# The last 1x1 convolution of a vision tower written with tokens as rows, with both norms and the gating logits taken from centred weights

## What is computed

```python
# tokenizer: patch embedding and a wavelet branch, gated, then three depthwise + 1x1 pairs
h = relu(dwconv(h, f1_dw, f1_pw, f1_pwb))
h = relu(dwconv(h, f2_dw, f2_pw, f2_pwb))
h = dwconv(loc + h, f3_dw, f3_pw, f3_pwb)          # 3x3 depthwise, then 1x1 with bias
t = transpose(h.reshape(B, D, -1), (0, 2, 1))
t = (t - mean(t)) / sqrt(var(t) + 1e-5) * ln_g + ln_b
h = concatenate([cls, t], axis=1)                  # 37 tokens an image
# the 37 tokens are all queries; there are no keys, so attention adds 0 @ proj_w.T + proj_b
h = layernorm(h + (zeros @ proj_w.T + proj_b))
v = clip(h @ v_w + v_b, -3, 3)                     # feeds a recurrence over the 37 tokens
logits = h @ gate_w + gate_b                       # 8 experts, the best two of each token
# experts: gelu(h @ w1[e] + b1[e]) @ w2[e] + b2[e], weighted; plus bk_scale * spectral part
h = layernorm(h + ffn(h))
```

## Time and profile before

| | |
|---|---|
| device time, median of 3 runs (lowest to highest) | 216.5 us (216.4 to 216.51) |
| the profiled execution: device time / span | 215.94 us / 214.1 us |
| busy: PE, DVE, ACT, POOL | 163.6, 103.6, 48.4, 84.0 us |
| DVE's last depthwise instruction ends | 74.57 us |
| DVE starts the logits (L698) | 93.59 us |
| first product of the experts starts (L998) | 118.29 us |
| granted clock of PE, mean | 0.891 |

### The profile page before, as it was taken

The page is one execution under the profiler, slowest core; times in us unless marked ns, Lnnn a source line. Parts: engine busy times, 40 slices in busy tenths (PEclk is TensorE's granted clock), DMA queues, the critical chain, the costliest instruction groups (busy, mean ns, idle before and its releaser), DMA issues.

```text
span 214.1 us, 2877 instructions
## 1 busy us (share of the span) xinstructions
PE 163.6 (76%) x934; PEld 132.9 (62%) x934; DVE 103.6 (48%) x304; ACT 48.4 (23%) x90; POOL 84.0 (39%) x203
## 2 busy tenths in 40 slices
PE   0999998977998872762207899999999999999100
PEld 0677764444555441562103799999999999999000
DVE  1109897699889949456800042322222223301385
ACT  0453343433311120233000222222221222221000
POOL 1699600000000013101775787878877323322111
PEclk9999999999999996555556999999999999999855
DMA  6992299999991000000222900000012100001412
GB/s 200 334 412 83 59 279 297 297 267 287 282 349 50 0 0 2 0 0 0 100 98 77 312 31 3 0 0 3 2 38 77 55 18 21 18 18 40 148 40 85
DMA packets 13632, 23.47 MB, mean 110 GB/s; under 512 B 1531, under 2 KB 10000, under 8 KB 13490
## 3 DMA queue, kind: packets, MB, share of 16 engines
q1 hardware_dynamic: 10862, 18.74, 28.4%
q0 software_dynamic: 1248, 2.76, 3.8%
q10 hardware_dynamic: 1508, 1.80, 2.6%
HBM read 17.98 MB, written 5.31 MB: 109 GB/s over the span
## 4 chain that ended last, share of the span: by engine, by line
PE 68%; DVE 11%; DMA 7%; POOL 5%; issue 5%; ACT 1%; POOLq 0%; DVEq 0%; ACTq 0%
PE ps L998 20%; PE ps L1008 15%; PE ps L845 8%; PE ps L853 7%; PE ps L854 5%; PE ps L899 5%; POOL slot_rows L405 4%; PE ps L833 3%; DMA w1t_s<-in_w1t 2%; DVE stats L642 2%; DVE conv L596 2%; DMA diag_s<-slot_results 2%; DVE conv L608 1%; POOL rstd L393 1%; DMA slot_rows<-sent,slots 1%
## 5 line engine op out<-in xcount | busy, mean ns | idle before, releaser
L998 PE MATMUL ps<-conv 128*128 128x128 f32 x384 | 45.7, 276 | 1.2 <-ACT conv L526 0.9
L998 PEld LDWEIGHTS ps<-conv 128*128 128x128 f32 x384 | 44.8, 192 | 1.9 <-ACT conv L526 1.4
L596 DVE SCALAR_TENSOR_TENSOR conv<-conv,vecs 128x240 f32<-128x240 f32 (+1 forms) x94 | 35.7, 443 | 7.9 <-ACT conv L463 7.4
L1008 PE MATMUL ps<-w_s,conv 128*128 x192 | 33.7, 326 | 0.0
L393 POOL TENSOR_TENSOR rstd<-var,neghalf 128x2 f32<-128x2 f32 (+1 forms) x6 | 4.9, 813 | 70.6 <-DVE var L648 70.6
L1008 PEld LDWEIGHTS ps<-w_s,conv 128*128 128x128 f32 x192 | 30.9, 190 | 0.0
L791 DVE COPY arena<-ps 128x192 f32<-128x192 f32 x16 | 5.7, 357 | 46.5 <-PE ps L1008 39.3
L413 POOL DMA_INDIRECT slot_results<-arena,home x16 | 17.5, 1091 | 25.5 <-DVE arena L791 23.2
L526 ACT COPY conv<-ps 128x256 f32<-128x256 f32 x16 | 6.0, 372 | 74.9 <-PE ps L989 74.9
L853 PE MATMUL ps<-conv,pw_s 128*128 128x288 f32 (+1 forms) x48 | 17.4, 445 | 5.5 <-DVE conv L608 3.8
L777 DVE COPY conv<-w_s 128x1536 f32 x16 | 15.6, 978 | 6.1 <-issue 6.0
(11 more groups left out here) (158 smaller groups left out, 188.5 us busy)
## 6 DMA issues: line engine op xcount, KB each, us to landing
w_s<-in_w SPq DMA_DIRECT2D x8, 576.0 KB, 14.8
w_s<-in_w SPq DMA_DIRECT2D x8, 384.0 KB
slot_rows<-zero SPq DMA_DIRECT2D x1, 2048.0 KB, 22.7
arena<-in_x SPq DMA_DIRECT2D x4, 432.0 KB, 9.5
w_s<-in_w SPq DMA_DIRECT2D x8, 192.0 KB
pw_s<-in_pw SPq DMA_DIRECT2D x1, 1152.0 KB, 11.4
arena<-slot_rows SPq DMA_DIRECT2D x1, 1024.0 KB, 8.0
w1t_s<-in_w1t ACTq DMA_DIRECT2D x1, 576.0 KB, 4.9
```

Of the source, the lines that this page charges most:

```text
L596: ins = nc.vector.scalar_tensor_tensor(out=o, in0=a, scalar=w, in1=o, op0=ALU.mult, op1=ALU.add)
L998: last = mm(p1_ps[i % 2][:, c * P:(c + 1) * P], w1_cur[:, i % 2, k * F + c * P:k * F + (c + 1) * P], xs[:, i % 2, k * P:(k + 1) * P], star ...
L1008: last = mm(y_ps[i % 2], hT[:, i % 2, k * P:(k + 1) * P], w2_flat[:, bass.ds(expert[i] * (FK * D) + k * D, D)], start=(k == 0), stop=(k == ...
```

## The change

The last 1x1 convolution no longer gives channels as rows that are then turned. The depthwise output `act_b` (tokens as columns) becomes the stationary operand and the weights the moving one, so that tokens come out as rows. Since a layer norm subtracts the mean over channels, the kernel subtracts it from the weights instead (`token_weights` on DVE, seven instructions, run in step (0, 0)). `wt` then holds three parts: the centred weights with a column for the epsilon (`CEN` = 193 columns), the centred weights times the gain, centred again (192), and these times the gate weights (9). The first norm's inverse deviation comes from the sum of squares of the first product (ACT, `Square` with an accumulated sum), and the second's from the sum of squares of `zc` = product times root plus `base` (the shift plus the attention bias, centred). The logits are `raw_ps` (nine more columns of the second product) times the first root, plus `base` times the gate weights (`s2`), times the second root. `bn_stats`, the turns of `act_a` and of `ht`, and the products L947 and L948 are dropped. ACT writes the ten tiles of `sent`. To prepare this PE turns `wt` and `base` with `shared` (the class tokens' row; four turns each) and multiplies them with the gate weights (eight products), between steps of the tokenizer; a row of ones in `act_b`, written by POOL, carries the bias of the convolution. The attention bias takes two products, after `branches`. `xf` has four tiles of columns, `full_tiles` shares the memory of `lgt`, POOL's memsets are five more, and DVE has two for `unit`.

```diff
+CEN, LGT = D + 1, 2 * D + 1
+TW = LGT + E + 1
...
+        tok_rows = [slice(0, min(P, NPX - t * P)) for t in range(NT)]
+        cen_ps = [ps[:, b, o:o + CEN] for b, o in ((0, 0), (0, 256), (2, 0), (3, 0), (4, 0))]
...
+        raw_ps = (psf[:, 512:1024].rearrange("p (t c) -> p t c", t=2)[:, :, D:TW - CEN], ps[:, 5:8, D:TW - CEN])
+        wturn_ps = (ps[:, 2, 0:2 * P], ps[LO, 3, 0:2 * P])
+        bturn_ps = (ps[:, 6, 0:2 * P], ps[LO, 7, 0:2 * P])
+        attn_ps = ps[:, 3, 0:D]
+        wl_ps = ps[:, 0, 0:4 * (E + 1)].rearrange("p (k e) -> p k e", k=4)
...
-            for k, grp in enumerate((0, 0, 1, 1)):
-                inverse_root(k, grp)
+            pool.wait_ge(padded, 11)
+            pool.wait_ge(pw_ev, 12)
+            nc.gpsimd.memset(act_b[DB:DB + 1, 1, :], 1.0).then_inc(ones_row, 1)
+            cr = slice(LAST, LAST + B)
+            pool.wait_ge(d_rows, 16)
+            pool.wait_ge(attn_rdy, 1)
+            pool.wait_ge(d_cls, 16)
+            pool.wait_ge(ones_row, 1)
+            nc.gpsimd.tensor_tensor(base[:], rowb[:, D:2 * D], attn[:], ALU.add).then_inc(base_rdy, 1)
+            pool.wait_ge(base_rdy, 1)
+            nc.gpsimd.tensor_tensor(shared[cr, :], cls_s[cr, :], attn[cr, :], ALU.add).then_inc(base_rdy, 1)
+            pool.wait_ge(bsum_rdy, 2)
+            nc.gpsimd.tensor_scalar(bsum[:], bsum[:], 1.0 / D, None, ALU.mult).then_inc(base_rdy, 1)
+            pool.wait_ge(base_rdy, 3)
+            nc.gpsimd.tensor_scalar(base[:], base[:], bsum[:, 0:1], None, ALU.subtract).then_inc(base_rdy, 1)
+            pool.wait_ge(base_rdy, 4)
+            nc.gpsimd.tensor_scalar(shared[:, :], shared[:, :], bsum[:, 1:2], None, ALU.subtract).then_inc(base_rdy, 1)
+            pool.wait_ge(base_rdy, 5)
+            for k, (c, ts, done) in enumerate(((0, slice(0, 2), 2), (1, slice(0, 2), 4), (0, slice(2, NT), 7),
+                                               (1, slice(2, NT), 10))):
+                if k:
+                    pool.wait_ge(root_rdy, k)
+                pool.wait_ge(sq_rdy, done)
+                nc.gpsimd.tensor_tensor(root[:, c, ts], sq[:, c, ts], neghalf[:, ts], ALU.pow).then_inc(root_rdy, 1)
             pool.wait_ge(d_clear, 16)
-            pool.wait_ge(padded, 6)
-            pool.wait_ge(ht_rdy, NT)
-            pool.wait_ge(copied, 1)
+            pool.wait_ge(padded, 11)
+            pool.wait_ge(copied, 2 * NT)
...
             branches(0)
             branches(1)
-            for f in range(3):
-                for g in range(2):
-                    fusion(f, g)
+            act.wait_ge(attn_mm, 1)
+            nc.scalar.copy(attn[:], attn_ps).then_inc(attn_rdy, 1)
+            fusion(0, 0)
+            act.wait_ge(wturn_mm, 1)
+            nc.scalar.copy(xf[:, 0, 0:2 * P], wturn_ps[0]).then_inc(xf_rdy, 1)
+            nc.scalar.copy(xf[LO, 1, 0:2 * P], wturn_ps[1]).then_inc(xf_rdy, 1)
+            fusion(0, 1)
+            act.wait_ge(bturn_mm, 1)
+            nc.scalar.copy(xf[:, 0, 2 * P:], bturn_ps[0]).then_inc(xf_rdy, 1)
+            nc.scalar.copy(xf[LO, 1, 2 * P:], bturn_ps[1]).then_inc(xf_rdy, 1)
+            fusion(1, 0)
+            fusion(1, 1)
+            act.wait_ge(wl_mm, 1)
+            nc.scalar.copy(wt[:, :, LGT:TW], wl_ps[:, 0:2, :]).then_inc(wl_rdy, 1)
+            nc.scalar.copy(s2[:], wl_ps[:, 2:3, :].to_broadcast([P, NT, E + 1])).then_inc(wl_rdy, 1)
+            act.wait_ge(wl_rdy, 2)
+            nc.scalar.copy(s2[LAST:LAST + B, NT - 1, :], wl_ps[LAST:LAST + B, 3, :]).then_inc(wl_rdy, 1)
...
+            scale = D ** -0.5
+            act.wait_ge(padded, 11)
+            def square(c, t, src, rows_):
+                nc.scalar.activation(sq_out[rows_, c, t, :], src, ACT.Square, scale=scale,
+                                     accum_out=sq[rows_, c, t:t + 1]).then_inc(sq_rdy, 1)
+            for g, tiles in enumerate(groups):
+                for t in tiles:
+                    act.wait_ge(cen_mm, max(t + 1, 2))
+                    square(0, t, cen_ps[t][tok_rows[t]], tok_rows[t])
+                for t in tiles:
+                    act.wait_ge(zc_rdy, t + 1)
+                    square(1, t, zc[:, t, :], A)
+            for c in range(2):
+                for t in range(NT):
+                    act.wait_ge(root_rdy, 2 if t < 2 else 4)
+                    nc.scalar.activation(sent[:, c, t, 0:D], zc[:, t, 0:D], ACT.Copy,
+                                         scale=root[:, 1, t:t + 1]).then_inc(copied, 1)
...
+            def token_weights():
+                last = pw_s[:, 5]
+                gain = rowb[:, 0:D].unsqueeze(1).to_broadcast([P, 2, D])
+                dve.wait_ge(d_pw, 16)
+                dve.wait_ge(d_rows, 16)
+                link(nc.vector.tensor_reduce(wsum[:, 0, :], last, AX.X, ALU.add))
+                link(nc.vector.tensor_scalar(wsum[:, 0, :], wsum[:, 0, :], 1.0 / D, None, ALU.mult))
+                link(nc.vector.tensor_tensor(wt[:, :, 0:D], last, wsum[:, 0, :].unsqueeze(2).to_broadcast([P, 2, D]),
+                                             ALU.subtract))
+                link(nc.vector.tensor_tensor(wt[:, :, CEN:LGT], wt[:, :, 0:D], gain, ALU.mult))
+                link(nc.vector.tensor_reduce(wsum[:, 1, :], wt[:, :, CEN:LGT], AX.X, ALU.add))
+                link(nc.vector.tensor_scalar(wsum[:, 1, :], wsum[:, 1, :], 1.0 / D, None, ALU.mult))
+                nc.vector.tensor_tensor(wt[:, :, CEN:LGT], wt[:, :, CEN:LGT],
+                                        wsum[:, 1, :].unsqueeze(2).to_broadcast([P, 2, D]), ALU.subtract).then_inc(wt_rdy, 1)
...
+                    if (f, g) == (1, 0):
+                        dve.wait_ge(base_rdy, 2)
+                        nc.vector.tensor_reduce(bsum[:, 0:1], base[:], AX.X, ALU.add).then_inc(bsum_rdy, 1)
+                        nc.vector.tensor_reduce(bsum[:, 1:2], shared[:, :], AX.X, ALU.add).then_inc(bsum_rdy, 1)
...
+                        if g == 0:
+                            token_weights()
...
+            dve.wait_ge(base_rdy, 5)
+            for k, tiles in enumerate(groups):
+                dve.wait_ge(root_rdy, 2 * k + 1)
+                for t in tiles:
+                    r = tok_rows[t]
+                    dve.wait_ge(tok_mm, max(t + 1, 2))
+                    nc.vector.scalar_tensor_tensor(out=zc[r, t, 0:D], in0=tok_ps[t][r, 0:D], scalar=root[r, 0, t:t + 1],
+                                                   in1=base[r, :], op0=ALU.mult, op1=ALU.add).then_inc(zc_rdy, 1)
+            def per_token(c):
+                return root[:, c, :].unsqueeze(2).to_broadcast([P, NT, E + 1])
+            dve.wait_ge(wl_rdy, 3)
+            for k, ts in enumerate((slice(0, 2), slice(2, NT))):
+                own(nc.vector.tensor_tensor(lgv[:, ts, :], raw_ps[k], per_token(0)[:, ts, :], ALU.mult))
+            dve.wait_ge(v_done, n)
+            link(nc.vector.tensor_tensor(lgv[:], lgv[:], s2[:], ALU.add))
+            dve.wait_ge(root_rdy, 4)
+            link(nc.vector.tensor_tensor(lgv[:], lgv[:], per_token(1), ALU.mult))
+            own(nc.vector.tensor_tensor(lg[:], lgv[:, :, 0:E],
                                         rowb[:, 2 * D:2 * D + E].unsqueeze(1).to_broadcast([P, NT, E]), ALU.add))
-            nc.vector.tensor_tensor(vt[:], lg_ps[:, :, E:E + 1].to_broadcast([P, NT, P // HB]),
+            dve.wait_ge(d_misc, 16)
...
-                if g == 0:
-                    pe.wait_ge(attn_rdy, 1)
...
-            mm(ps[:, 3, 0:D], zero[:, 0:P], proj_s[:, 0, :], start=True, stop=False)
-            mm(ps[:, 3, 0:D], zero[LO, 0:P], proj_s[LO, 1, :], start=False, stop=False)
-            mm(ps[:, 3, 0:D], ones[:], projb_s[:], start=False, stop=True).then_inc(attn_mm, 1)
             pe.wait_ge(d_pw, 16)
             branches(0)
             branches(1)
-            for f in range(3):
-                for g in range(2):
-                    if (f, g) in PE_HELPS:
-                        taps(f, g)
-                    fusion(f, g)
-            for group, done in (((0, 1), 22), ((2, 3, 4), 24)):
-                pe.wait_ge(pw_ev, done)
-                if group[0] == 0:
-                    pe.wait_ge(d_misc, 16)
-                for t in group:
+            pe.wait_ge(d_proj, 32)
+            pe.wait_ge(zeroed, 1)
+            pe.wait_ge(unit_rdy, 2)
+            mm(attn_ps, zero[:, 0:P], proj_s[:, 0, :], start=True, stop=False)
+            mm(attn_ps, unit[:], proj_s[:, 1, :], start=False, stop=True).then_inc(attn_mm, 1)
+            pe.wait_ge(ones_row, 1)
+            fusion(0, 0)
+            taps(0, 1)
+            pe.wait_ge(attn_rdy, 1)
+            pe.wait_ge(wt_rdy, 1)
+            for k in range(2):
+                nc.tensor.transpose(wturn_ps[0][:, k * P:(k + 1) * P], wt[:, k, CEN:CEN + P], id_s[:])
+                last = nc.tensor.transpose(wturn_ps[1][:, k * P:(k + 1) * P], wt[:, k, CEN + P:LGT], id_s[:])
+            last.then_inc(wturn_mm, 1)
+            fusion(0, 1)
+            pe.wait_ge(xf_rdy, 2)
+            taps(1, 0)
```

(51 more changed lines are left out.)

126 lines of the change are left out of this document (55 added, 71 removed).

## The result

The changed kernel took **209.6 us** in the median of four runs (207.0 to 210.8), beside 216.45 us of the kernel before on the same chip: a ratio of 0.964, 95% interval 0.956 to 0.973. It is faster; 207.6 us was predicted, with a range from 205.4 to 211.3. The runs lie apart: 207.0, 209.6, 209.6 and 210.8. The profiled execution is the one of 210.8 us, so its trace holds losses that a typical run has only in part.

The account below looks back on a forecast made before the run. No engine is full in the 19.02 us relay of latencies from tokenizer to logits; it becomes 7.75: 11.3 gained, 2.4 given back ahead, 8.9 net, 216.5 to 207.6 us, range 205.4 to 211.3.

Parts of the forecast that it names:

- Part 1: Weights prepared on DVE in step (0, 0): seven instructions, 3.25 us against 2.89 idle; +0.1 us into f = 1.
- Part 2: Turns and reductions between tokenizer steps: reductions fit DVE's idle 0.81 us; four turns at 0.23 each make PE 0.45 us late.
- rival (c): PE hides its weight loads, 0.65 us a pair; DVE ends the tokenizer, the turns fit: 205.6 us, chance 0.08.
- Part 3: Eight nine-column products ahead of `fusion(1, 1)`: 1.75 us plus 0.1 wait; that 1x1 starts 1.9 us late, at 65.2.
- Part 4: Token rows of group 0: four pairs at 0.85 us, 3.4 in all; PE ends the tokenizer 2.4 us later.
- Part 5: New relay from tokenizer to logits: squares 0.5 us each, logits at 84.7; stage 7.75 us instead of 19.02.
- a sign of being wrong: Listed in the prediction: it is wrong if the square's accumulated sum on ACT is a second instruction of its own.
- Part 6: Behind the logits: ten copies end near 88.4 us, exponential near 89.9, nothing delays the scatter; warm-up shifts along.
- Rival (e): PE's clock rises later before the experts; missing by 3 us loses 1.5 us: 209.1 us, chance 0.06.
- Rival (g): PE's clock falls to half inside the tokenizer through gaps behind new waits: near 230 us for five half steps, chance 0.04.
- that part moves as a block with whatever releases it: From the first expert product on, PE multiplies back to back, nothing the change touches lies there; that part only shifts.

Follow-up runs that it names:

- again: The changed kernel measured once more with nothing changed: 208.48 us, ratio 0.962; its trace is of the run of 207.19 us.
- 5: Kernel of 4 with POOL's addition for `base` held back until ACT's first copy of step (0, 0): 206.67 us, ratio 0.957.
- 9: Kernel of 4 with turns of `base`/`shared` and four gate products moved later, their additions on DVE in (1, 0), reductions in (1, 1): 204.19 us.
- experiment 7: Changed kernel with the long warm-up of 3, logits made the old way behind the last root, prepared turns and gate products removed: 212.56 us, ratio 0.981.
- 3: Changed kernel with PE's warm-up before the experts of eleven products instead of three, six between the loads of expert numbers: 207.49 us, ratio 0.955.
- 4: Changed kernel with the eleven-product warm-up of 3 and the eight gate products reading 107 columns instead of nine: 206.41 us, ratio 0.955.
- 12: Kernel of 9 plus twelve one-column memsets on POOL that nothing waits for: 205.10 us, ratio 0.946.

## Why the prediction was right, and where it was not

The forecast of faster and the range held, and 207.6 was 2.0 us low. Two errors stand against each other in that. From (0, 0) to the logits the change gained 10.4 us without the dent, for 8.9 forecast: up to the end of the tokenizer it took 29.31 us in "again" (46.06 to 75.37) for 30.28 (46.67 to 76.95), and from there to the logits 7.30 for 7.75. Behind the logits 2.2 to 3.1 us were lost, where the prediction took all as constant, and the dent, where it came, took 1.65. So that the middle of the range came near is in part luck.

- **Part 1.** The seven instructions took 0.55, 0.17, 0.56, 0.56, 0.55, 0.17, 0.56, as estimated; L725 starts at 39.58, 0.41 after L624 in the earlier trace rows (0.35 forecast). POOL's row of ones was ready 0.3 us before (0, 0) needed it. What was missed is beside it: POOL's addition of `base` and its overlap with DVE, 0.6 us (experiments 5 and 9). No term of the sum had it.
- **Part 2.** The four turns stand 0.11 to 0.16 us apart, not 0.23. The clock doesn't explain it: it was full at that row too (1.00 from 77 to 78 us before the change), but there each turn of 128 rows alternates with one of 64, 0.26 and 0.20 apart. What makes the difference is open. The turns fitted into PE's free time, 5.35 us from (0, 1) to (1, 0) for 5.34 before, so the 0.45 was not paid, as rival (c) had it. From (0, 0) to (1, 0) it took 11.65 us, for 11.82 forecast; what was paid there is the overlap of part 1.
- **Part 3.** Eight products in 1.81 us for 1.75 forecast. The 1x1 of (1, 1) started at 65.38 for 65.2, and 6.66 us behind that of (1, 0), for 6.7. The price was right; what it did to the clock was not foreseen.
- **Part 4.** Pairs of token rows start 0.66 to 0.73 apart, not 0.85, close to rival (c)'s 0.65. Four pairs took 2.75 us up to the taps, 0.65 less than forecast, the three of the relay some 0.3 less, at 0.74 to 0.80. DVE had no idle time before its last additions (77.17 above), so DVE ended the tokenizer, and not PE: that too is rival (c), which had 0.08 and a stage shorter by 10.9 us. It was nearer to the stage's 10.4 than the sum's 8.9.
- **Part 5.** The square is 0.33 to 0.36 and its accumulated sum a second instruction of 0.18 to 0.20, which the prediction had named as a sign of being wrong. It cost nothing beyond the 0.5 taken: the second starts before the first ends, so the pair is done after 0.42 to 0.46 us, and the next square starts 0.33 to 0.36 after the one before. Logits at 85.32 in the trace with the dent, 82.67 in that without, for 84.7.
- **Part 6.** The copies ended at 87.88, 3.7 us before the slots; the squares needed no table load, and the one for the exponential began at 87.90. The Trainium skill ("ScalarE: Activation LUTs", section "Table sets: the hidden batching unit") would have asked for one before the squares, as square is not among the functions it names for every set; the trace has none there. The 0.7 us of the slower scatters stood in no term.
- **Rival (e), the clock's later rise,** had 0.06 and came true in both traces of the changed kernel: the first expert group took 5.49 and 4.51 us, 1.6 to 2.6 more than 2.94. It was argued from a single trace, in which the warm-up ended 0.65 us ahead of the rows. The shorter relay by itself moves the warm-up and the rows alike. But counted from the logits the warm-up began at 18.85 us, and at 19.30 before, and the rows came at 24.5 to 24.6, and at 23.8 before, which the slower scatters account for. So PE stood idle for 1.58 and 1.98 us instead of 0.65. Whether that gap alone costs the clock isn't shown: in the trace of after the clock had not risen before it. The Trainium skill's rule, that this moment isn't tied to the kernel's start and moves from run to run ("TensorE: Matmul & The Clock Gate", section "The HAM clock gate (the "warmup" mystery)"), fits: in two traces of one kernel the first group differs by 1 us here.
- **Rival (g), the clock falling inside the tokenizer,** was right as to place and wrong as to size: it came for one 1x1, 1.65 us, not for five half steps. It came with PE busy, behind the narrow products, and not behind a gap as (g) argued; only the dent of experiment 7 stands behind a gap.

The step that failed is "that part moves as a block with whatever releases it": the 95.81 us from the first expert product on became 97.3 to 97.8, and the 24.70 before it 25.4 to 25.8. In sum, for the profiled execution: 47.07 - 46.67 = 0.4 for the head, 0.22 for the stretch to the logits (1.65 for the dent, less 1.43 for pairs, turns and hand-overs), 1.06 to the first expert product, 2.0 behind it; 3.7 of the 3.8 us between 207.0 and 210.8.

What is shown for the dent: it was in two of three traces with eight narrow products ahead of (1, 1), and in none of eight with four of them or with wide ones, which chance alone would give in about one case of eighteen (3 / 55). Between 3 and 4, which differ in the width alone, the upper cluster of times goes; but the times are weaker evidence than the traces, since single runs as high also came with wide products (208.57 in 5, 207.84 in 12, whose trace has no dent). That the narrow products bring it is thus supported, not proven.

## What to carry to other kernels

When a relay of latencies is changed, look at what PE does just behind it: a warm-up that used to be enough may now end too early or raise the clock too late for the first real products. Here 1.3 to 2.6 us of a gain of 10.4 were lost so in the three traces with the short warm-up, and were had back by more such products, spread over the wait. And price an operation put on POOL together with what it does to DVE beside it: 1.28 us on POOL and 0.6 on DVE against 0.34 on DVE alone.

## What the runs showed of the hardware

- With PE busy without a gap, its clock fell from 2.4 to 1.2 GHz behind the eight products of nine columns in two of three traces (about 65 us), and was back by 70 us; with 107 columns, or four such products, it stayed at 2.4 GHz there in eight traces.
- In "again" the clock was up at 105 us, within the warm-up, and down again at 108 us behind 1.98 us of idle PE and the first turn of rows. In the trace of after a warm-up of 4.18 us did not raise it. With eleven products over some 11 us the first expert group took 2.94 us in all ten traces, one of them of the kernel before.
- An ACTIVATE of 128x193 with an accumulated sum (0.33 to 0.36 us) is followed by an instruction of its own, 0.18 to 0.20 us, to read it; the two overlap, 0.42 to 0.46 us together.
- One POOL addition of 128x192 with two inputs took 1.06 to 1.28 us and stretched DVE's work beside it by 0.6 to 0.7 us, whether that was two scalings (0.64 to 1.25) or ten taps (3.70 to 4.37).
